# Grouped-query attention stage: two moves in the engines' orders, and one load block for x and the stage's weights

## The reference

```python
qkv = jnp.einsum('bsh,oh->bso', x, w_qkv)
q, k, v = jnp.split(qkv, [H * D, (H + HKV) * D], axis=-1)
q = _layernorm(q, qn_g, qn_b); k = _layernorm(k, kn_g, kn_b)      # per head
q = q * cos + _rotate_half(q) * sin; k = k * cos + _rotate_half(k) * sin
k = jnp.repeat(k, rep, axis=1); v = jnp.repeat(v, rep, axis=1)
scores = jnp.where(causal, -jnp.inf, einsum(q, k) / sqrt(D))
attn = einsum(softmax(scores), v)                                  # then @ w_o.T, added to x
```

## Time and profile before

| quantity | value |
| --- | --- |
| median of three runs | 3246.2 us |
| profiled execution, its span | 3244.57 us, 3242.8 us |
| PE, DVE, ACT, POOL busy, share of the span | 82%, 63%, 49%, 42% |
| x, first weight piece: DMAs issued at | 1.23 us, 16.94 us |
| first PE instruction | 59.79 us |
| attention stage, loop in steady state | some 100 to 900 us |
| 400 to 500 us: PE, DVE, ACT, POOL busy of 100 us | 86.1, 85.4, 56.4, 80.8 |
| granted clock of TensorE from 200 to 900 us | 1.00 |

### The profile page before, as it was taken

How to read it: one execution, slowest core, us unless ns; L and a number is a source line. 1 busy time by engine, 2 the same in 40 slices (tenths; PEclk the granted TensorE clock), 3 DMA queues, 4 the chain that set the end, 5 groups by cost and what they waited for, 6 DMA issues and landing times. The chain is left out here.

```text
span 3242.8 us, 85996 instructions
## 1 busy us (share of the span) xinstructions
PE 2653.5 (82%) x33006; PEld 1936.8 (60%) x33006; DVE 2034.8 (63%) x3734; ACT 1574.7 (49%) x2946; POOL 1358.5 (42%) x1483
## 2 busy tenths in 40 slices
PE   1888888888858888867677779999999999996565
PEld 1667777777732222224466667888888888885333
DVE  4888888888857888848577743434334343434676
ACT  2555555555527777731233314344443434442565
POOL 1888888888832333314222212222222222220665
PEclk9899999999978999979799989999999999998576
DMA  3000000000013333300000020000000000000000
GB/s 119 2 1 0 0 0 0 0 0 0 0 36 91 92 92 92 90 13 0 27 26 26 26 68 6 7 5 7 6 7 7 6 7 5 7 4 28 13 16 23
DMA packets 94784, 77.50 MB, mean 24 GB/s; under 512 B 17520, under 2 KB 88560, under 8 KB 93424
## 3 DMA queue, kind: packets, MB, share of 16 engines
q1 hardware_dynamic: 94576, 74.35, 7.5%
HBM read 55.97 MB, written 17.04 MB: 23 GB/s over the span
## 5 line engine op out<-in xcount | busy, mean ns | idle before, releaser
L1319 DVE TENSOR_REDUCE x_mx<-x_ps 128x2 f16<-128x512 f32 x512 | 330.9, 682 | 49.7 <-PE x_ps L1383 47.5
L1288 ACT ACTIVATE x_e<-x_ps 128x512 f32<-128x512 f32 x512 | 292.0, 596 | 49.7 <-PE x_ps L1387 33.8
L365 POOL TENSOR_TENSOR x1s<-x1s,x1mx 128x1024 f32<-128x1024 f32 x32 | 60.8, 1901 | 541.9 <-DVE x1mx L361 541.9
L1383 PE MATMUL x_ps<-x_k,x_q 32*128 32x256 f16 x1024 | 196.1, 285 | 81.2 <-ACT x_e L1288 50.7
L1642 ACT ACTIVATE x_q<-x_ps,x_q_bias,x_q_scale 128x128 f32<-128x128 f32 x512 | 185.7, 467 | 158.3 <-PE x_ps L105 158.3
L435 ACT CAST x1oh<-x_ps 128x1024 f16<-128x1024 f32 x64 | 64.7, 1012 | 329.9 <-PE x_ps L427 329.9
L103 PE MATMUL a_ps<-ln_xha,a_wq 128*128 128x128 f16 x1024 | 180.2, 222 | 51.2 <-ACT a0v L605 44.1
L1383 PEld LDWEIGHTS x_ps<-x_k,x_q 32*128 32x128 f16 x1024 | 58.3, 93 | 263.4 <-DVE x_mx L1319 130.6
L554 POOL TENSOR_TENSOR a_w<-a_qsw,a_tab 128x512 f32<-128x512 f32 x128 | 176.7, 1380 | 57.4 <-ACT a_qsw L615 56.1
L1387 PE MATMUL x_ps<-x_q,x_k 32*128 32x256 f16 x1024 | 197.8, 287 | 1.7 <-ACT x_e L1288 1.4
L105 PE MATMUL x_ps<-x_chi,x_w 128*128 128x128 f16 x1024 | 181.3, 221 | 17.2 <-issue 17.2
(11 more groups left out here) (360 smaller groups left out, 9110.7 us busy)
## 6 DMA issues: line engine op xcount, KB each, us to landing
x_q<-x_q_rows SPq DMA_DIRECT2D x32, 256.0 KB, 2.8
x_k<-x_k_rows SPq DMA_DIRECT2D x32, 256.0 KB, 3.1
a_stage<-in_x_w SPq DMA_DIRECT2D x32, 256.0 KB, 2.6
x_vt<-in_ctx_v SPq DMA_DIRECT2D x32, 144.0 KB, 2.3
x_wt<-in_x_wt SPq DMA_DIRECT2D x4, 1028.0 KB, 5.7
x_all<-in_x SPq DMA_DIRECT2D x8, 512.0 KB, 8.0
x_cf<-in_ctx SPq DMA_DIRECT2D x32, 128.0 KB, 2.1
x_q_rows<-x_xhl SPq DMA_DIRECT2D x32, 128.0 KB, 1.7
```

The source lines that it names most:

```text
L1288: act.activation(e[:, u % ES].rearrange("p c n -> p (c n)"), s2_ps(u), ACT.Exp, scale=XT ** -0.5).then_inc(e_ready, 1)
L1319: dve.reduce_max(mx[:, p % 2, c:c + 2], s1_ps(u), AX).then_inc(mx_ready, 1)
L1383: return pe.matmul(s1_ps(u)[:, c], q[r, p % 4, g, c * P:(c + 1) * P], k[r, p % 4, g], start=True, stop=True)
```

## The change

Four edits, two in the loop and two at the start:

1. ACT: in a step, the value copy and the second high part come ahead of the exponential, not behind it.
2. DVE: the second low part comes ahead of the denominators.
3. `load_resident` loads only the identity. The new `load_gqa` loads the attention weights, x and the three constants in one block, each piece into a buffer of its own, and x's last seven pieces last. The block doesn't wait for those; DVE waits for them in step 1, SP in the attention block.
4. In `load_gqa` the low parts of the query and key weights are computed by POOL (before by DVE), from weights that DVE has already scaled and centred in one instruction; the others stay on DVE.

```diff
         def _(sp):
             sp.dma_start(m.ident[:, :], m.d["ident"]).then_inc(id_in, 16)
-            for s in range(0, TILES, 4 if TILES >= 4 else TILES):
-                ...
-            sp.wait_ge(x_in, 16 * (TILES // min(4, TILES)))
+            sp.wait_ge(id_in, 16)
...
+def load_gqa(m, d, wq, wk, wv, wo, rope, gb, mask, x_first, x_in, const_in):
+        sizes = (("q0", 2048), ("q1", 2048), ("k", 1024), ("v", 1024), ("o0", 2048), ("o1", 2048))
+        ...
+        centre = ("q0", "q1", "k")
+        @block.sync       # q0, q1, k, x 0, v, o0, rope, gb, mask, o1, x 1 to 7
+        def _(sp):
+            ...
+            sp.wait_ge(const_in, 48)
+        @block.scalar
+        def _(act):
+            for i, (n, (hi, lo)) in enumerate(order):
+                if n in centre:
+                    act.wait_ge(centred, i + 1)
+                    act.copy(hi, st[n][:, :]).then_inc(high_done, 1)
+                else:
+                    act.wait_ge(loaded[n], 16)
+                    act.activation(hi, st[n][:, :], ACT.Copy, scale=WS).then_inc(high_done, 1)
+        @block.vector
+        def _(dve):
+            def centre_heads(i, n):
+                ...
+                dve.reduce_sum(mean[:, 0:heads], w, AX).then_inc(summed, 1)
+                dve.tensor_scalar(mean[:, 0:heads], mean[:, 0:heads], WS / P, None, ALU.mult).then_inc(mean_set, 1)
+                dve.scalar_tensor_tensor(w, w, WS, spread(mean[:, 0:heads], P), ALU.mult, ALU.subtract).then_inc(centred, 1)
+            ...
+            for i, (n, (hi, lo)) in enumerate(order):
+                if n not in centre:
+                    dve.wait_ge(high_done, i + 1)
+                    dve.scalar_tensor_tensor(lo, st[n][:, :], WS, hi, ALU.mult, ALU.subtract).then_inc(wide_low_done, 1)
+        @block.gpsimd
+        def _(pool):
+            for i, (n, (hi, lo)) in enumerate(order):
+                if n in centre:
+                    pool.wait_ge(high_done, i + 1)
+                    pool.tensor_tensor(lo, st[n][:, :], hi, ALU.subtract).then_inc(low_done, 1)
...
                     square(t + 1, 1)
-                at_.exponential(act, t)
-                if has_next:
                     value(t + 1, 1 - p)
                 if before:
                     at_.high(act, t - 1, 1, not has_next)
+                at_.exponential(act, t)
...
-                at_.denominator(dve, ch, t)
                 if before:
                     at_.low(dve, t - 1, 1, not has_next)
+                at_.denominator(dve, ch, t)
```

More of the change, by code:

```diff
@@ L127, in load_resident @@
         sem = ctx.enter_context(Semaphores(nc, "in_"))
-        x_in, id_in = sem("x_in"), sem("id_in")
+        id_in = sem("id_in")
         block = ctx.enter_context(nc.Block())
@@ L133, in _ @@
             sp.dma_start(m.ident[:, :], m.d["ident"]).then_inc(id_in, 16)
-            for s in range(0, TILES, 4 if TILES >= 4 else TILES):
-                n = min(4, TILES)
-                sp.dma_start(m.x_all[:, s:s + n, :],
-                             m.d["x"][s * P:(s + n) * P, :].rearrange("(t p) d -> p t d", p=P)).then_inc(x_in, 16)
-            sp.wait_ge(x_in, 16 * (TILES // min(4, TILES)))
+            sp.wait_ge(id_in, 16)
         @block.vector
@@ L464, in add, with load_x @@
         upd.then_inc(self.x_done, 1)
+X_PIECE = 4
+def load_gqa(m, d, wq, wk, wv, wo, rope, gb, mask, x_first, x_in, const_in):
+    nc = m.nc
+    with ExitStack() as ctx:
+        sizes = (("q0", 2048), ("q1", 2048), ("k", 1024), ("v", 1024), ("o0", 2048), ("o1", 2048))
+        st = {n: ctx.enter_context(nc.sbuf_tensor("stage_a0" + n, [P, c], F32)) for n, c in sizes}
+        mean = ctx.enter_context(nc.sbuf_tensor("mean_a0", [P, 16], F32))
+        sem = ctx.enter_context(Semaphores(nc, "a0w_"))
+        loaded = {n: sem("loaded_" + n) for n, _ in sizes}
+        summed, mean_set, centred = sem("summed"), sem("mean_set"), sem("centred")
+        high_done, low_done, wide_low_done = sem("high_done"), sem("low_done"), sem("wide_low_done")
+        flat = lambda w: w[:, :, :].rearrange("p c n -> p (c n)")
+        q, k, v = ([flat(w[i]) for i in range(2)] for w in (wq, wk, wv))
+        half = lambda a, i: a[:, 2048 * i:2048 * (i + 1)]
+        order = (("q0", [half(a, 0) for a in q]), ("q1", [half(a, 1) for a in q]), ("k", k), ("v", v),
+                 ("o0", [half(a[:, :], 0) for a in wo]), ("o1", [half(a[:, :], 1) for a in wo]))
+        centre = ("q0", "q1", "k")
+        block = ctx.enter_context(nc.Block())
+        @block.sync
+        def _(sp):
+            def load_x(i, landed):
+                rows = m.d["x"][i * X_PIECE * P:(i + 1) * X_PIECE * P, :]
+                sp.dma_start(m.x_all[:, i * X_PIECE:(i + 1) * X_PIECE, :],
+                             rows.rearrange("(t p) d -> p t d", p=P)).then_inc(landed, 16)
+            sp.dma_start(st["q0"][:, :], half(d["a0_q"], 0)).then_inc(loaded["q0"], 16)
+            sp.dma_start(st["q1"][:, :], half(d["a0_q"], 1)).then_inc(loaded["q1"], 16)
+            sp.dma_start(st["k"][:, :], d["a0_k"]).then_inc(loaded["k"], 16)
+            load_x(0, x_first)
+            sp.dma_start(st["v"][:, :], d["a0_v"]).then_inc(loaded["v"], 16)
+            sp.dma_start(st["o0"][:, :], half(d["a0_o"], 0)).then_inc(loaded["o0"], 16)
+            sp.dma_start(rope[:, :, :], d["rope"]).then_inc(const_in, 16)
+            sp.dma_start(gb[:, :], d["a0_gb"]).then_inc(const_in, 16)
+            sp.dma_start(mask[:, :], d["causal"]).then_inc(const_in, 16)
+            sp.dma_start(st["o1"][:, :], half(d["a0_o"], 1)).then_inc(loaded["o1"], 16)
+            for i in range(1, TILES // X_PIECE):
+                load_x(i, x_in)
+            sp.wait_ge(const_in, 48)
[11 more added lines that the diff above has]
+            def centre_heads(i, n):
+                w = st[n][:, :].rearrange("p (h d) -> p h d", d=P)
+                heads = w.shape[1]
+                dve.wait_ge(loaded[n], 16)
+                dve.reduce_sum(mean[:, 0:heads], w, AX).then_inc(summed, 1)
+                dve.wait_ge(summed, i + 1)
+                dve.tensor_scalar(mean[:, 0:heads], mean[:, 0:heads], WS / P, None, ALU.mult).then_inc(mean_set, 1)
+                dve.wait_ge(mean_set, i + 1)
+                dve.scalar_tensor_tensor(w, w, WS, spread(mean[:, 0:heads], P), ALU.mult, ALU.subtract).then_inc(centred, 1)
+                dve.wait_ge(centred, i + 1)
+            for i, n in enumerate(centre):
+                centre_heads(i, n)
+            for i, (n, (hi, lo)) in enumerate(order):
[8 more added lines that the diff above has]
+                    pool.tensor_tensor(lo, st[n][:, :], hi, ALU.subtract).then_inc(low_done, 1)
@@ L484, in attention_gqa @@
         wo = [sb(f"wo{i}", [P, HEADS * DM], F16) for i in range(2)]
[L485 to L488, removed]
+        rope = sb("rope", [P, 2, SEQ])
+        gb = sb("gb", [P, 2, 4])
+        mask = sb("mask", [P, SEQ])
+        x_first, x_in, const_in = sem("x_first"), sem("x_in"), sem("const_in")
+        load_gqa(m, d, wq, wk, wv, wo, rope, gb, mask, x_first, x_in, const_in)
         ln = LayerNorm(m, ctx, sem, "a0", ps[:, 0, :])
         at_ = Attend(m, ctx, sem, "a0", ps, wo, NK)
-        rope = sb("rope", [P, 2, SEQ])
-        gb = sb("gb", [P, 2, 4])
         tab = sb("tab", [P, 7, SEQ])
@@ L495, in attention_gqa @@
         bq2 = sb("bq2", [P, 2, SEQ])
-        mask = sb("mask", [P, SEQ])
         u = sb("u", [P, 2, HEADS, SEQ])
@@ L512, in attention_gqa @@
         s2m = sb("s2m", [P, 2 * KV, SEQ])
-        const_in, tab_set = sem("const_in"), sem("tab_set")
+        tab_set = sem("tab_set")
         chain, pool_chain = sem("chain"), sem("pool_chain")
@@ L535, in _ @@
         def _(sp):
[L536 to L539, removed]
+            sp.wait_ge(x_in, 16 * (TILES // X_PIECE - 1))
         @block.gpsimd
@@ L658, in tables @@
                 cos, sgn = rope[:, 0, :], rope[:, 1, :]
-                dve.wait_ge(const_in, 48)
                 for i, (c, swap, b) in enumerate(((QC, QW, BQ), (KC_, KW, BK))):
@@ L700, in head @@
                 tables()
+                dve.wait_ge(x_first, 16)
                 ln.stats(dve, ch, 0, 0)
@@ L729, in step @@
                 if further(t):
+                    if isinstance(t, int) and t == 1:
+                        dve.wait_ge(x_in, 16 * (TILES // X_PIECE - 1))
                     ln.stats(dve, ch, t + 2, p)
```

## The result

The changed kernel takes 3229.2 us in the median of six runs, the kernel before 3247.2 us beside it. One of the six runs was disturbed (4622.7 us); without it the others are 3223.0 to 3238.6 us with a median of 3226.6, and the ratio is 0.9936, with a 95% interval of 0.9916 to 0.9955, or 21 us (15 to 27). Forecast were 3196 us, with a range of 3182 to 3212.

What follows compares the result with a forecast made beforehand. PE was taken as the busiest engine, stopping three times a tile. Start 20 + loop 30 = 50 us off the profiled 3244.6 gave 3194.6; with 1.6 for the median, 3196 us, range 3182 to 3212.

Steps and rivals of the forecast that it cites:

- The start: Load block up to the first row statistics: 20 us earlier (13 to 25).
- the walk with turns: Load block: DVE and POOL hold their shared SBUF port in turns, so the block ends at 34.8 us, not 29.7.
- ACT and DVE in the loop: Attention tile: exponential 0.1 us late, squares 2 earlier by 1.2, norm by 0.55, rows' low part at 532.1 against 533.22.
- The norm at 0.4: DVE's `xn` in the loop: goes ahead of POOL's `normalise` and takes 0.4 us instead of 1.15.
- no PE wait on `a0v`: PE in the loop: queries 3 no longer wait for the value copy, 1.4 us earlier.
- PE's `keys`, and with them the next tile, start 1.1 us earlier: PE in each attention tile: the rows' earlier low part moves keys and the following tile forward by 1.1 us.
- PE's wait on the rows' low part still there at about 2 us: Sign expected in the profile after: PE's stop ahead of the next rows in the loop stays, about 2 us.
- 30 x 1.0 = 30 us: Attention loop: 1.0 us gained in each of 30 tiles, 30 us in all (17 to 39).
- The stops only change their name: Rival, chance 0.13: PE's loop gain is lost again ahead of the rows' low part; the start's 20 alone, 3226 us.
- All of it arrives: Rival, chance 0.07: both PE stops in the loop vanish and nothing replaces them; 84 us off, 3162 us.
- no turns: Rival, chance 0.15: DVE and POOL work side by side in the load block; 24 + 30 us off, 3192 us.
- the exponential becomes late: Rival, chance 0.02: ACT's exponential waits behind a high part needing PE's values; at 3 us, 3285 us.

Runs made afterwards that it cites:

- e3: Changed kernel plus six 512-column matmuls, result not read, in PE's pause behind the next rows' transposes; ratio 0.9898 to the kernel before.
- e4: Kernel before with only the new start, plus six unread matmuls behind the next rows' transposes on PE; ratio 1.0030 to the kernel before.
- e10: Changed kernel plus three unread matmuls in PE's pause and 23 short ones behind the attention stage; 3181.7 us, ratio 0.9792 to the kernel before.
- e5: Changed kernel plus three unread 512-column matmuls in PE's pause behind the next rows' transposes; ratio 0.9934 to the kernel before.
- e8: Changed kernel with DVE's move taken back, so only ACT's new order stays in the loop; ratio 1.0012 to the kernel before.
- e11: Changed kernel with ACT's move taken back, so only DVE's new order stays in the loop; ratio 1.0034 to the kernel before.

## Why the prediction was wrong

- **The start: right.** 18.0 us against 20 (13 to 25), and the walk with turns (35.9 against 34.8) was the right one; without turns it would have been 29.7. What was held first was not the wide subtraction, as the walk had it, but the small scaling ahead of it.
- **ACT and DVE in the loop: right in the main.** The norm at 0.4, the add held by POOL's `normalise`, no PE wait on `a0v`, the rows' low part 1.1 us earlier against the end of `subtract_max` (6.8 us behind it, before 7.9): all measured. The exponential was 0.2 us late, not 0.1, and the way from it to the low part shrank by 1.4 us, not 1.2.
- **The step that failed: "PE's `keys`, and with them the next tile, start 1.1 us earlier".** The keys do (7.3 us behind `subtract_max` instead of 8.5). "And with them the next tile" took for granted that PE's work behind the pause lasts as long as before. I had named that pause as staying ("PE's wait on the rows' low part still there at about 2 us") and had not asked what a single pause of that length, in place of three shorter ones, does to the clock. It falls for 3.4 us in most tiles, so 1.7 us of PE work at full speed are lost in each such tile; with five of seven tiles that is 1.2 us a tile against a gain of 1.1. So the term "30 x 1.0 = 30 us" measured -1 us (816.2 before, 817.4 after). e3 shows what it was lost to: the pause filled, the rest of the loop as it was, clock 1.00, and the loop gives 816.2 - 782.0 = 34 us, where 30 had been forecast. e4, with the same matmuls and the old order, gives nothing in the loop.
- **The rivals.** "The stops only change their name" gave 3226 and the measured time is near it, but by luck: DVE and POOL did not take the gain back; a gain of 1.1 us and a loss of 1.2 to the clock happen to cancel. "All of it arrives", "no turns" and "the exponential becomes late" did not happen.
- **Not settled:** what exactly makes the clock fall. With the new order it fell behind three of four pauses of 2.2 to 2.5 us and behind five of 29 of 1.8 (e10; one of 29 in e5); in e8 it fell at all 28 of 2.4 us, in e11 at one of 29 of 2.3 to 2.4, and in e3's cross attention at five of 13 of 3.2 us and more. Length alone does not decide.

## What to carry to other kernels

When a change merges short idle times of TensorE into one longer one, price the work behind it at the lower clock as well, and look at the granted clock tile by tile before and after; a few matmuls whose result nobody reads can be cheaper than the pause, as three or six were here, and one was not. A gain in one stage must be checked stage by stage: moving the code of a later hardware loop by a few dozen instructions cost up to 30 us or saved 23, more than the change itself brought.

## What the hardware showed that was not expected

- Three matmuls (0.6 us) in a pause of 2.4 us saved 32 us in 31 tiles (817.4 to 785.3; 24 us in e10, 793.1); one saved nothing (816.5).
- The cross attention's loop cost 947 to 948, 968 to 973, 994 or 995 to 1003 us with identical code, by the number of PE instructions ahead of it (moved by 64, 0, 18 and 36). The waits marked issue differ (0, 16 to 17, 27 and 43 to 45 us), and with them the clock, which adds up to 12.5 us of PE busy time to the changed kernel's.
- DVE's 0.17 us scaling of 16 means, whose operand and result lie in SBUF, was held for 3.6 us by a POOL instruction that had begun 0.34 us earlier, so a DVE instruction with a single tensor operand, and of 16 numbers, was held too.
